# Residual rows of a recurrence: added by an identity product on TensorE and copied back by ScalarE, where VectorE added them

## The reference

```python
xz = x @ W_in; x_proj, z = split(xz)             # x is the normalised input, 256 -> 2 x 512
x_conv = silu(causal_conv4(x_proj) + conv_b)
dt_in, B = split(x_conv @ W_x)
dt = softplus(dt_in @ W_dt + b_dt)
h = h * exp(dt * A) + dt * B * x_conv            # per channel (512) and state (16), over time
y = (h.sum(states) + x_conv * D) * silu(z)
x = x + y @ W_out                                # residual
```

## Time and profile before

| | us |
|---|---|
| runs, median (lowest to highest of 3) | 826.59 (825.5 to 828.36) |
| profiled execution | 824.91, of it the span 823.1 |
| recurrence, first to last scan | 48.7 to 427.1 |
| busy in the span: PE, DVE, ACT, POOL | 637.5, 601.7, 421.6, 453.6 |

### The profile page before, as it was taken

One profiled execution on the slowest core, in us unless ns is written; L12 is line 12 of the kernel. 1 busy time (PEld: TensorE's weight loads), 2 busy tenths in 40 slices (PEclk: granted clock), 3 DMA queues, 4 the chain that ended last, 5 costly groups with the idle time before them and its releaser, 6 DMA issues. The chain is left out here.

```text
span 823.1 us, 11006 instructions
## 1 busy us (share of the span) xinstructions
PE 637.5 (77%) x3196; PEld 400.5 (49%) x3196; DVE 601.7 (73%) x1009; ACT 421.6 (51%) x744; POOL 453.6 (55%) x324
## 2 busy tenths in 40 slices
PE   4569857996499854653379799999999988899950
PEld 2123212341134210210038699998989964588840
DVE  5767787799977999997987566668777665344316
ACT  2557898587966898553425334434334220244420
POOL 3058698798986989995942212212334236046550
PEclk9789986999689985675589899999999999999985
DMA  7143342334334344464202113313413049655418
GB/s 195 34 109 92 76 99 64 97 87 102 88 79 99 78 105 103 100 186 103 67 0 87 41 61 111 131 46 128 144 54 106 15 133 325 139 152 150 134 27 300
DMA packets 70584, 87.43 MB, mean 106 GB/s; under 512 B 18197, under 2 KB 47320, under 8 KB 70526
## 3 DMA queue, kind: packets, MB, share of 16 engines
q1 hardware_dynamic: 54782, 67.26, 30.7%
q10 hardware_dynamic: 12000, 11.28, 4.3%
q0 software_dynamic: 3744, 8.19, 2.9%
HBM read 36.54 MB, written 18.66 MB: 67 GB/s over the span
## 5 line engine op out<-in xcount | busy, mean ns | idle before, releaser
L262 POOL TENSOR_TENSOR b_in<-u_rep,b_rep 128x1024 f32<-128x1024 f32 x128 | 299.0, 2361 | 72.3 <-DMA dt_rep<-dt 30.1
L477 DVE TENSOR_TENSOR_SCAN h<-ps,hlast,b_in 128x512 f32<-128x512 f32 x256 | 306.3, 1265 | 22.0 <-ACT ps L383 11.1
L383 ACT ACTIVATE ps<-dt_rep,neg_a 128x512 f32<-128x512 f32 x256 | 171.4, 686 | 75.5 <-DVE h L477 60.2
L615 PE MATMUL ps<-h,pick 128*32 128x512 f32 x512 | 84.9, 742 | 70.4 <-DVE h L477 70.0
L512 PE MATMUL ps<-xnT,w_in 128*128 128x512 f32 x128 | 67.8, 677 | 17.6 <-ACT xnT L308 10.3
L615 PEld LDWEIGHTS ps<-h,pick 128*32 128x32 f32 x512 | 11.0, 118 | 134.9 <-DVE h L477 130.5
L917 POOL DMA_INDIRECT rows_by_token<-yt,yrow x46 | 44.9, 975 | 52.4 <-DVE yrow L1254 25.3
L1061 DVE TENSOR_TENSOR p_lo<-ps,p_hi 128x512 fp32r<-128x512 f32 x64 | 35.1, 587 | 42.8 <-ACT p_hi L928 42.6
L1292 PE MATMUL ps<-v_hi,p_hi 128*128 128x256 f32 x208 | 59.7, 287 | 1.2 <-DVE x_res L1158 1.2
L1292 PE MATMUL ps<-v_hi,p_lo 128*128 128x256 f32 x208 | 58.5, 281 | 0.0
L1292 PE MATMUL ps<-v_lo,p_hi 128*128 128x256 f32 x208 | 58.5, 281 | 0.0
(11 more groups left out here) (228 smaller groups left out, 1289.3 us busy)
## 6 DMA issues: line engine op xcount, KB each, us to landing
u_rep<-u SPq DMA_DIRECT2D x256, 64.0 KB, 2.0
dt_rep<-dt SPq DMA_DIRECT2D x248, 64.0 KB, 2.0
mask_sb<-in_mask_BxSxS_ik_dram SPq DMA_DIRECT2D x16, 800.5 KB, 4.5
xt<-rows_by_expert SPq DMA_DIRECT2D x46, 129.0 KB
rows_by_token<-pad ACTq DMA_DIRECT2D x4, 1024.0 KB, 5.1
yb<-rows_by_token SPq DMA_DIRECT2D x4, 512.0 KB, 5.2
yb<-rows_by_token ACTq DMA_DIRECT2D x4, 512.0 KB, 5.9
x_res<-in_x_dram SPq DMA_DIRECT2D x1, 1536.0 KB, 8.7
```

The source lines that it names most:

```text
L262: pool.tensor_tensor(b_in[:, (t - 1) % NB:(t - 1) % NB + 2, :], u_rep[:, n % 2, j - 1:j + 1, :], b_rep[:, q % 2, g, :].unsqueeze(1).to_bro ...
L383: act.activation(psA[:, t % NDA, :], dt_rep[:, n % 2, j, :], ACT.Exp, scale=neg_a[:, k:k + 1]).then_inc(exp_ready, 1)
L477: dve.tensor_tensor_scan(h[:, QC * (s % NH) + j, :], psA[:, t % NDA, :], b_in[:, t % NB, :], hlast[:, k:k + 1], ALU.mult, ALU.add).then_in ...
L615: last = pe.matmul(psY[32 * j:32 * j + 32, :], pick[:, :], h[:, QC * (s % NH) + j, :], start=False, stop=(g == NG - 1))
```

## The change

Each `project` gets a fifth product, identity x rows of x_res, into the same accumulation. So psF holds the sum of residual and output product, and ScalarE copies it into x_res. The copies stand in ScalarE's slots 30, 31, 33 and 34 (`ACT_RES`), after the exponential of that t and ahead of the other front work of the slot. VectorE's twelve additions of chunks 0 to 2 are gone; those of the last chunk stay. `project` also waits for the load of the later rows of x (`x_rest`).

```diff
-DVE_MOM, DVE_RES, DVE_DT, DVE_NEXT = -18, (26, 27, 29, 30), (53, 55, 60, 62), 40
+DVE_MOM, ACT_RES, DVE_DT, DVE_NEXT = -18, (30, 31, 33, 34), (53, 55, 60, 62), 40
...
                 for c, f in front_slots(t):
+                    if f in ACT_RES and c >= 2:
+                        i = ACT_RES.index(f)
+                        act.wait_ge(proj_ps, CHT * (c - 2) + i + 1)
+                        act.activation(x_res[:, CHT * (c - 2) + i, :], psF[:, i % 2, 0:DM], ACT.Copy).then_inc(x1_done, 1)
                     if c < NQ:
                         front(c, f)
...
                 for c, f in front_slots(t, 2):
-                    if f in DVE_RES:
-                        i = DVE_RES.index(f)
-                        residual(CHT * (c - 2) + i, psF[:, i % 2, 0:DM])
                     if f == DVE_MOM and c < NQ:
...
             def project(q, t):
                 pe.wait_ge(gated, KM * (q + 1))
                 pe.wait_ge(s_wout, 16)
+                pe.wait_ge(x_rest, 16)
                 for m in range(KM):
-                    last = pe.matmul(psF[:, t % 2, 0:DM], zs[:, q % 2, m, t * P:(t + 1) * P], w_out[:, m, :],
-                                     start=(m == 0), stop=(m == KM - 1))
-                last.then_inc(proj_ps, 1)
+                    pe.matmul(psF[:, t % 2, 0:DM], zs[:, q % 2, m, t * P:(t + 1) * P], w_out[:, m, :], start=(m == 0), stop=False)
+                pe.matmul(psF[:, t % 2, 0:DM], ident[:, :], x_res[:, CHT * q + t, :], start=False, stop=True).then_inc(proj_ps, 1)
```

## The result

The changed kernel takes 828.92 us in the median (7 runs, 827.68 to 831.5), the one before 826.59 (7 runs, 823.26 to 828.36). The ratio is 1.0045, 95% interval 1.0029 to 1.0062, so slower by 3.7 us (2.4 to 5.1). The two medians themselves lie only 2.3 us apart. The profiled execution's span grew by 4.1 us, 823.1 to 827.2. The forecast was +4.6.

A forecast was written before the change was run, and what follows sets the result against it. Four engines nearly full, with TensorE gapless and ScalarE in a backlog at the residual additions; 2.3 + 2.3 + 0 = +4.6 us for the three chunks gives 829.5 profiled, 831.2 us on the median, own range 829 to 833.5.

The forecast's parts named there:

- TensorE's products alone: Rival: only the added products count and z waits for nothing; gate at 184.6, +1.1 us a chunk, 828.8 us; chance 0.13.
- TensorE's products: Step: each projection gains one 128x256 product, +0.45 us a projection, 1.8 us a chunk.
- Copy 1 holds up the Silu: Second chunk, ScalarE: copy 1 waits for projection 1 until 169.95; table load at 170.25 in place of 168.53, +1.7.
- z products and gate: Second chunk: first z product waits for copy 2 until 176.5 (+3.0); gate at 185.8 in place of 183.47, +2.3 us.
- SyncE's block n=6: Second chunk: exponential t=79 ends later, so SyncE's next block starts 2.25 us late.
- No delay is taken back between the chunks: After the second chunk's gate: VectorE and SyncE's copies stay late, so the third chunk starts 2.3 us late.
- The chain to the end has no slack: From SyncE's copies at 270.57 through GpSimd to VectorE's release at 386.61: delay carried through, ended 4.6 us later.
- The fourth chunk is free: Residual additions from 346.35: price 0, hidden by the 5.82 us wait before 386.61; without that cover a 3.3 us gain.
- The bound for dearer copies: Upper bound with ScalarE's copies at 590 ns instead of 378: the sum becomes 5.8 us instead of 4.6.
- VectorE alone: Rival: VectorE alone decides and each residual group gives its gain, 6.3 us in all, 820.3 us; chance 0.07.
- that the delay is taken back: Rival: gate waits at 232 and 257 in the third chunk's front absorb it; about 0 remains, 826.6 us; chance 0.10.
- The clock didn't fall in the new gap: Rival: TensorE's clock falls after 1.2 us of standing; some 7 us a chunk, 845 us; 0.09 including a dearer chain.

The follow-up runs named there:

- e2: Changed kernel without the identity product, ScalarE copying the bare projection: ratio 1.0063 to the kernel before (+5.2 us), gate t=66 to t=82 22.75 us.
- e4: Changed kernel with ScalarE's large Silu in slot 27 instead of 31, ahead of the copies: ratio 1.0015 to the kernel before, gate t=66 to t=82 22.15 us.
- e5: Kernel before with the Silu in slot 27: ratio 1.0002 to the kernel before, gate t=66 to t=82 21.10 us.
- e7: Kernel before with SyncE issuing the attention's ten loads after block n=15: ratio 0.9924 to the kernel before (6.3 us gained).
- e8: Kernel before with the change (identity product, ScalarE's copies) in the fourth chunk only: ratio 0.9994 to the kernel before (-0.5 us).
- e9: Kernel before with attention's loads after block n=15 and the change in the fourth chunk only: ratio 0.9921 to the kernel before (-6.5 us).
- e12: Kernel before, attention's loads after block n=15, change in fourth chunk only, copies in slots 32, 33, 35, 36: ratio 0.9911 to before, median 818.47 us.
- e11: Kernel before with the Silu in slot 27 and the attention's loads after block n=15: ratio 0.9932 to the kernel before (-5.6 us).
- e3: Kernel before with the 12 additions of the first three chunks left out, no replacement: ratio 0.9993 to the kernel before, median 823.81 us.

## Why the prediction was right

The direction and the place hold, and the size roughly. On the total I had some luck. The forecast of 831.2 us added 1.7 us, the distance of the median from the profiled execution before; in the changed kernel the profiled execution is itself the median, 828.92, which belongs beside the 829.5 forecast for it. And 828.92 is just below the forecast's own range (829 to 833.5) and next to the 828.8 of the rival with TensorE's products alone: the total can't tell the two apart. What does is the gate at 186.00 where that rival has 184.6, the copy that waits, and e2 and e4. By its steps:

- **TensorE's products**: 0.45 us each, measured 0.43.
- **ScalarE's copies**: 378 ns, measured 0.38 where they waited and 0.36 where not.
- **Copy 1 holds up the Silu**: copy at 169.95 and table load at 170.25, measured 169.94 and 170.34. e4 and e5 show the cause: with the Silu elsewhere the wait of the z products vanishes in the one kernel, and nothing happens in the other.
- **z products and gate**: 176.5 and 185.8, measured 176.61 and 186.00; +2.3 a chunk foreseen, +2.53 measured. Of the 0.2 missing, 0.1 is the table load, which came 0.1 later after the copy, and 0.1 the first two z products with the sum behind them (176.61 to 181.24, where it was 173.52 to 178.04).
- **SyncE's block n=6**: +2.25, measured +2.34.
- **The third chunk repeats it**: 23.62 us from gate to gate after 23.61.
- **No delay is taken back between the chunks**: this held. The gate of t=114 waited 4.69 us where it had waited 4.22, so the shift was 2.99 there, and block n=10 was 5.33 us late where the prediction had 4.55. But 0.46 us of this need not be the change's: they come from the clock that TensorE was granted during the sum ahead of that gate, 0.75 in the kernel before, 0.57 in the changed one, and 0.50 in e7, whose second chunk is the same as the kernel before's and whose gate waited 4.76. This sum in the three:

```profile
231.23 1.39 PE L615 MATMUL ps<-h,pick 128*32 128x512 f32 x8
```
```profile
233.76 1.85 PE L616 MATMUL ps<-h,pick 128*32 128x512 f32 x8
```
```profile
232.45 1.94 PE L614 MATMUL ps<-h,pick 128*32 128x512 f32 x8
```

- **The chain to the end has no slack**: in the main right, off by its size. Block n=13 was 5.08 us late, block n=14 4.36 (366.83 after 362.47): the DMA issues between them took 0.7 us less than in the profile of before. The issues vary by so much from run to run. So the 4.35 us in the end are near the forecast partly by luck: some 0.5 us from the granted clock were added on the way and 0.7 us of issues taken off.
- **The fourth chunk is free**: VectorE's longer wait in e8 bears this out. But the gain without the cover, 3.3 us for the additions and waits, left out a cost. From the gate of t=194 to that of t=210 the changed kernel gained 1.5 us (22.97 to 21.46), and e9 gained 2.7 on e7. ScalarE's copies, waiting up to 3.1 us for the projections, hold up the exponentials there too. e12 shows 3.9 against e7, once the copies stand later. This distance doesn't repeat as the other ones do: the four kernels that have VectorE's additions and no product (before, e5, e7, e11) lie between 22.97 and 23.48, and the first three projections took 5.66 us before, at a granted clock of 0.96, and 6.19 in e7, at 0.87, where the second chunk's took 5.45.
- **The bound for dearer copies** was added up a little too high: with a copy of 590 ns copy 1's step grows by 0.22 and copy 2's end by 0.21 more, 0.43 us a chunk, which makes 5.5 and not 5.8.

The rivals: VectorE alone is refuted by e2 and e3; TensorE's products alone by e2 and e4; that the delay is taken back by the profile. The clock didn't fall in the new gap: between 164 and 187 us, which holds the new wait of 1.20 us, the granted clock was 1.00, its upper level. Even behind e2's wait of 2.06 us the eight records of the z products took 3.70 us, as they do in the changed kernel.

```profile
164.00:187.00 23.00, 21.74 (x98) 11.46 (x98) 19.11 (x18) 17.43 (x30) 18.79 (x8) 1.00 0.31 76
```

The Trainium skill (Perfetto Trace Analysis, "Optimizing Scalar/DVE Operations") says that handing work from a saturated VectorE to ScalarE may make sense. Here it did not pay: e3 shows that even leaving this work out for free was worth only 0.66 us in the second chunk and as much in the third.

## What to carry to other kernels

Before moving work off the busiest engine, leave it out altogether and look at the next wait: if another engine's chain is ready only 0.7 us earlier, that is all there is to gain. Work that is moved brings its wait along, and in an in-order queue this wait is paid by whatever stands behind; here a copy of 0.38 us cost 1.8 us because a Silu with two table loads stood there. With the long instruction put ahead of the copies the cost fell from 2.52 to 1.06 us a chunk (e4); what was left was TensorE's added work, and no place of the copies removes that. Later slots for the copies helped in the fourth chunk (e12); no run shows them in the second and third.

## What the runs showed that was not expected

SyncE's queue is a bound of its own: a block's 32 DMA issues take 20.2 us (2.49 us for four), VectorE's 16 scans 18.9, and ten other loads of 8.2 us ahead of block n=14 cost 6.3 us of the total (e7). And the issue times scatter: most groups of four took 2.41 to 2.50 us, but single ones 2.7 to 3.8 in every profile (3.76 before, 3.46 in the changed kernel). By the rows this moves SyncE's chain by up to about a microsecond, and it hides effects that the distance between two gates shows to 0.02.
